# Four small reorderings in a routed MLP-and-adapter kernel: the first rows' turns, a split result sum, tail sums by matmul, two more unused products

## The reference

```
q, k, v = x@Wq, x@Wk, x@Wv ; attn = softmax(q k^T / 16) ; a = (attn v)@Wp + bp
cms     = gelu(a@cW1 + cb1)@cW2 + cb2 + one_hot(code)          # 256 -> 1024 -> 256
mod     = gelu([a, cms]@mW1 + mb1)@mW2 + mb2                    # 512 -> 1024 -> 256
x1      = clip(x + cms + mod, 0, 1)
for layer in 3 adapters:   # weights chosen by the batch's role, 3 roles
    u  = gelu(x@W_down[role] + b_down)@W_up[role] + b_up        # 256 -> 128 -> 256
    x  = layernorm(x + u) * gamma[role] + beta[role]
```

## Time and profile before

| | |
|---|---|
| timed runs | 366.13 us median (365.42 to 367.71) |
| profiled execution | 363.89 us, its span 362.1 us |
| TensorE matmul busy | 348.7 us, 96% of the span |
| TensorE weight load | 282.9 us, 78% |
| VectorE | 197.0 us, 54% |
| ScalarE | 166.4 us, 46% |
| GpSimd | 62.0 us, 17% |
| granted TensorE clock | 9 (full) in all 40 slices |
| busy tenths of TensorE, first and last slice | 7 and 4, 9 in nearly all between |

### The profile page before, as it was taken

One profiled execution on the slowest core, in us unless ns is written; L12 is line 12 of the kernel. 1 busy time (PEld: TensorE's weight loads), 2 busy tenths in 40 slices (PEclk: granted clock), 3 DMA queues, 4 the chain that ended last, 5 costly groups with the idle time before them and its releaser, 6 DMA issues.

```text
span 362.1 us, 6606 instructions
## 1 busy us (share of the span) xinstructions
PE 348.7 (96%) x2232; PEld 282.9 (78%) x2232; DVE 197.0 (54%) x477; ACT 166.4 (46%) x333; POOL 62.0 (17%) x94
## 2 busy tenths in 40 slices
PE   7889999999999999999999999999999999999994
PEld 6677688677876867888786777877899999989962
DVE  5057365420332746763535766554579777553584
ACT  3465685432652555452326454443455554533421
POOL 2700230000040101001311111003322025100231
PEclk9999999999999999999999999999999999999999
DMA  6663799175020223220076797602856543298001
GB/s 209 202 229 119 200 106 162 11 213 130 2 58 0 60 80 97 69 79 0 29 242 159 208 264 241 172 29 80 207 151 191 160 107 98 66 295 310 16 2 44
DMA packets 30646, 46.14 MB, mean 127 GB/s; under 512 B 4779, under 2 KB 15348, under 8 KB 30612
## 3 DMA queue, kind: packets, MB, share of 16 engines
q1 hardware_dynamic: 28852, 41.72, 42.6%
q0 software_dynamic: 1392, 3.80, 3.6%
q10 hardware_dynamic: 368, 0.20, 0.2%
HBM read 43.60 MB, written 4.48 MB: 133 GB/s over the span
## 4 chain that ended last, share of the span: by engine, by line
PE 85%; ACT 5%; DVE 4%; issue 3%; POOL 2%; DMA 1%; POOLq 0%; DVEq 0%; ACTq 0%
PE bank L312 11%; PE bank L314 10%; PE bank L313 10%; PE bank L1353 8%; PE bank L1358 8%; PE bank L1354 7%; PE bank L1277 4%; PE bank L1397 4%; PE bank L1376 3%; PE bank L1228 2%; PE bank L1267 2%; PE bank L1248 2%; ACT h_full L760 2%; PE bank L1428 2%; ACT h_hi L764 1%
## 5 line engine op out<-in xcount | busy, mean ns | idle before, releaser
L760 ACT ACTIVATE h_full<-bank,bias 128x512 f32<-128x512 f32 (+1 forms) x80 | 48.2, 602 | 114.4 <-PE bank L314 109.6
L985 DVE TENSOR_TENSOR h_lo<-h_full,h_hi 128x512 fp32r<-128x512 f32 (+1 forms) x80 | 46.7, 584 | 65.1 <-ACT h_hi L764 63.6
L683 POOL TENSOR_TENSOR rstd<-moments,minus_half 128x1 f32<-128x1 f32 x39 | 24.3, 624 | 174.2 <-DVE moments L1039 174.2
L764 ACT ACTIVATE h_hi<-h_full 128x512 fp32r<-128x512 f32 (+1 forms) x80 | 43.7, 546 | 2.6
L1031 DVE TENSOR_TENSOR window_y<-bank,window_x 128x256 f32<-128x256 f32 x39 | 16.5, 423 | 42.6 <-PE bank L1376 34.8
L1353 PE MATMUL bank<-h_hi,m_hi 128*128 128x512 f32 (+1 forms) x80 | 31.1, 397 | 0.4 <-ACT h_hi L764 0.3
L1353 PE MATMUL bank<-h_hi,c_hi 128*128 128x512 f32 (+1 forms) x80 | 30.8, 395 | 0.1
L312 PE MATMUL bank<-at_hi,m_hi 128*128 128x512 f32 (+1 forms) x80 | 29.5, 369 | 0.0
L312 PE MATMUL bank<-at_hi,c_hi 128*128 128x512 f32 (+1 forms) x80 | 29.4, 367 | 0.0
L314 PE MATMUL bank<-at_lo,c_hi 128*128 128x512 f32 (+1 forms) x80 | 27.8, 348 | 0.0
L314 PE MATMUL bank<-at_lo,m_hi 128*128 128x512 f32 (+1 forms) x80 | 27.8, 347 | 0.0
(11 more groups left out here) (216 smaller groups left out, 717.9 us busy)
## 6 DMA issues: line engine op xcount, KB each, us to landing
adapter_w<-packed_w SPq DMA_DIRECT2D x48, 256.5 KB, 3.5
adapter_rows<-packed_rows SPq DMA_DIRECT2D x36, 256.0 KB, 3.7
mixed_w<-packed_w SPq DMA_DIRECT2D x12, 256.5 KB, 4.6
stage<-in_L_cond_mW SPq DMA_DIRECT2D x6, 512.0 KB, 4.7
stage<-in_L_cond_cW SPq DMA_DIRECT2D x4, 512.0 KB, 6.5
last_w<-packed_w SPq DMA_DIRECT2D x2, 769.5 KB, 5.8
up_bias<-in_L_cond_b_up SPq DMA_DIRECT2D x12, 128.0 KB, 5.5
adapter_rows<-packed_rows SPq DMA_DIRECT2D x24, 64.0 KB, 3.2
```

The source lines that it names most:

```text
L683: pool.tensor_tensor(slot.rstd[:, :], slot.moments[:, 1:2], minus_half[:, :], ALU.pow)\
L760: act.activation(h_full[:, n % 2, rows], bank[n % 2][:, rows], ACT.Gelu, bias=bias[:, b:b + 1])\
L764: act.activation(h_hi[:, n % 2, rows], h_full[:, n % 2, rows], ACT.Copy).then_inc(h_hi_ready, 1)
L985: dve.tensor_tensor(h_lo[:, n % 2, rows], h_full[:, n % 2, rows], h_hi[:, n % 2, rows].bitcast(F32), ALU.subtract).then_inc(h_lo_ready, 1)
```

## The change

- In `core`, `D 7` comes right behind `D 6`; before, `Ha 8` stood between them. `C` is one place earlier for that.
- In the start, `half_part("X", 0)` comes ahead of `fold_weights(1)` and the bias turn, and `half_part("X", 1)` ahead of `half_part("Y", 0)`, on TensorE and ScalarE. `keep_busy(1)` is added ahead of the wait for `earlier_ready`, and the one of 64 columns becomes one of 128.
- Group 2's `F` and `E` run in two halves of 256 rows (F, E, F, E), so `x1_needed` of windows 8 and 9 asks for the first half only. Counts of `mod_summed` and `x1_ready` change to suit.
- Tails: `last_sum` on VectorE is gone. TensorE puts `up_bias` into the sum bank with an identity product (`last_bias`), `last_first_sum` is two plain products with the identity as the moving side that add to it, and layer 0's `last_residual` is gone. Tail one's `last_bias`, `last_first_sum` and `last_down` stand behind `Hb 9` of group 4, ahead of `D 8`; before, the latter two stood behind `D 8`.

```diff
-        core += [("D", HB - 2), ("Ha", HB), ("D", HB - 1), ("C", 0), ("Ha", HB + 1), ("Hb", HB), ("Hb", HB + 1)]
+        core += [("D", HB - 2), ("D", HB - 1), ("C", 0), ("Ha", HB), ("Ha", HB + 1), ("Hb", HB), ("Hb", HB + 1)]
...
+        def sum_parts(g):
+            return 2 if g + 1 in CARRIED and GROUPS[g][1] == GR else 1
+        def summed(g):
+            return VB * sum(sum_parts(n) for n in range(g))
...
+            n, (first, rows) = next((n, group) for n, group in enumerate(GROUPS) if (w + 1) * P <= sum(group))
+            part = ((w + 1) * P - first - 1) * sum_parts(n) // rows
+            return PRIMED + summed(n) + VB * (part + 1)
...
+                if step in ("F", "E"):
+                    share = size // sum_parts(g)
+                    for part_n in range(sum_parts(g)):
+                        rows = slice(part_n * share, (part_n + 1) * share)
...
-            def last_sum(tail):
-                dve.wait_ge(tail.loaded, 16 * tail.loads)
-                dve.wait_ge(tail.turned, 1)
...
-                dve.tensor_tensor(tail.x[:, :], tail.sum_bank[:, 0:V], tail.up_bias[:, :], ALU.add).then_inc(tail.x_ready, 1)
...
             keep_busy(2)
...
             pe.matmul(bank[4][0:B, 0:1], role_row[:, 1, :], ones[0:1, 0:1], start=True, stop=True).then_inc(roles_turned, 1)
+            keep_busy(1)
             pe.wait_ge(earlier_ready, 1)
...
-            keep_busy(1, P // 2)
+            keep_busy(1)
...
+            def last_bias(n):
+                tail = last[n]
+                pe.wait_ge(tail.loaded, 16 * tail.loads)
+                pe.matmul(tail.sum_bank[:, 0:V], ident[:, :], tail.up_bias[:, :], start=True, stop=False)
...
-                    ins = pe.transpose(tail.sum_bank[:, vb * P:(vb + 1) * P], xT[:, vb, columns(w)], ident[:, :])
-                ins.then_inc(tail.turned, 1)
+                    pe.matmul(tail.sum_bank[:, vb * P:(vb + 1) * P], xT[:, vb, columns(w)], ident[:, :],
+                              start=False, stop=False)
...
+            half_part("X", 0)
             pe.wait_ge(wT_copied, 3)
...
-            half_part("X", 0)
+            half_part("X", 1)
             half_part("Y", 0)
-            half_part("X", 1)
             half_part("Y", 1)
...
-                if g == NM - 1 and step == ("D", HB):
+                if g == NM - 1 and step == ("Hb", HB + 1):
                     pe.wait_ge(cms_copied, VB * NM)
-                    pe.wait_ge(last[0].loaded, 16 * last[0].loads)
+                    last_bias(0)
                     pe.wait_ge(x1_ready, x1_needed(LAST[0]))
+                    last_first_sum(0)
                     last_down(0, 0)
-                    last_first_sum(0)
                 if g == NM - 1 and step == ("D", HB + 2):
-                    last_residual(0, 0)
                     last_up(0, 0)
```

More of the change, by code:

```diff
@@ L467, in go @@
             def go():
-                engine.wait_ge(tail.x_ready, tail.base + LAYERS + 1)
+                engine.wait_ge(tail.x_ready, tail.base + LAYERS)
                 for q, place in zip(quarters, places):
@@ L806, in last_part @@
                 if stage_name == "turn":
-                    act.wait_ge(tail.turned, layer + 1)
+                    act.wait_ge(tail.turned, layer)
                     act.activation(tail.xT[:, :, :], two(tail.turn_bank[:, 0:V]), ACT.Copy).then_inc(tail.xT_ready, 1)
@@ L1007, in part @@
                     dve.wait_ge(base_ready, VB * (g + 1))
[L1008 to L1015, removed]
+                if step in ("F", "E"):
+                    share = size // sum_parts(g)
+                    for part_n in range(sum_parts(g)):
+                        rows = slice(part_n * share, (part_n + 1) * share)
+                        cols = slice(first + part_n * share, first + (part_n + 1) * share)
+                        if step == "F":
+                            for vb in range(VB):
+                                dve.scalar_tensor_tensor(cms[:, vb, rows], result_banks(g, HB)[vb][:, rows],
+                                                         bias[:, MB2 + vb:MB2 + vb + 1], xT[:, vb, cols], ALU.add, ALU.add)\
+                                    .then_inc(mod_summed, 1)
+                        if step == "E" or sum_parts(g) > 1:
+                            for vb in range(VB):
+                                dve.wait_ge(mod_summed, summed(g) + VB * part_n + vb + 1)
+                                dve.tensor_scalar(xT[:, vb, cols], cms[:, vb, rows], 0.0, 1.0, ALU.max, ALU.min)\
+                                    .then_inc(x1_ready, 1)
             def before(wave, spot):
@@ L1078, in last_norm @@
                 dve.wait_ge(tail.rstd_ready, tail.base + layer + 1)
+                if layer == 0 and tail.left:
+                    dve.wait_ge(*tail.left)
                 dve.scalar_tensor_tensor(tail.x[:, :], tail.y[:, :], tail.rstd[:, :], tail.rows[layer][:, 1, :],
@@ L1099, in _ @@
                     part("E", 0, g - 1)
-                if g + 1 in CARRIED and step == ("F", 0):
+                if g + 1 in CARRIED and step == ("F", 0) and sum_parts(g) == 1:
                     part("E", 0, g)
@@ L1173, in _, with keep_busy @@
             pe.wait_ge(ident_ready, 1)
-            def keep_busy(n, columns=P):
+            def keep_busy(n):
                 for _ in range(n):
-                    pe.matmul(bank[6][:, 0:columns], ident[:, :], ident[:, 0:columns], start=True, stop=True)
+                    pe.matmul(bank[6][:, 0:P], ident[:, :], ident[:, :], start=True, stop=True)
             keep_busy(2)
@@ L1446, in last_residual @@
                 tail = last[n]
-                pe.wait_ge(tail.x_ready, tail.base + layer + 1)
+                pe.wait_ge(tail.x_ready, tail.base + layer)
                 pe.matmul(tail.sum_bank[:, 0:V], ident[:, :], tail.x[:, :], start=True, stop=False)
@@ L1517, in _ @@
             last_down(one, 1)
+            pe.wait_ge(gelu_done, PRIMED + 2 * HB * NM)
+            last_bias(two_)
             last_up(one, 1)
-            pe.wait_ge(x1_ready, PRIMED + VB * NM)
-            pe.wait_ge(gelu_done, PRIMED + 2 * HB * NM)
+            last_bias(three)
+            pe.wait_ge(x1_ready, PRIMED + summed(NM))
             pe.wait_ge(emptied[6], used[6])
@@ L1523, in _ @@
             for n in (two_, three):
-                pe.wait_ge(last[n].loaded, 16 * last[n].loads)
                 last_down(n, 0)
                 last_first_sum(n)
-            for n in (two_, three):
-                last_residual(n, 0)
-                last_up(n, 0)
+            last_up(two_, 0)
+            last_up(three, 0)
             last_turn(one, 2)
```

23 lines of the change are left out of this document (8 added, 15 removed).

## The result

The change made the kernel slower: 369.45 us median (368.74 to 369.86, four executions) against 365.77 us (365.00 to 367.71) of the kernel before on the same chip, a ratio of 1.0113 with an interval of 1.0071 to 1.0155 (the medians alone give 1.010). Forecast was 367.6, in a range to 369.8. The profiled execution took 369.24 us, span 367.4, where that of before took 363.89 and 362.1: +5.3 us between the two profiles. The mean granted clock of TensorE is 0.982 to 0.987 in all four executions; in the profile of before it was 1.00.

What follows compares the result with a forecast made beforehand. TensorE's work plus its gaps was taken as the bound (85% of the last chain). Terms +0.8 + 0.3 - 0.5 - 0.2 + 1.4 - 0.4 + 0.1 gave +1.5 us on the median 366.13: 367.6 us, range 365.1 to 369.8.

Steps and rivals of the forecast that it cites:

- start, order: First turn to first scores: the second fold no longer hides behind the gather, +0.8 us, bounds 0 and +2.1.
- tail one's entry: Group 4: the bias product ahead of `D 8` waits for the last of tail one's loads, +1.4 us.
- start: order and unused products: Start up to the first scores: new order +0.8 us and added unused products +0.3 us.
- `D 7` ahead of `Ha 8`: Group 0: `cms` leaves its banks earlier, so TensorE's wait at `Hb 8` shrinks, -0.5 us; nothing in other groups.
- `F` and `E` in halves: End of group 2: window 8's down product no longer waits, but a wait returns later, -0.2 us.
- residual gone: Group 4: the residual product that goes from `D 10` gives -0.4 us.
- tails: Tails: two bias products come in and VectorE's three sums go, +0.1 us, bounds -0.3 and +0.4.
- +0.3 for the added products: Start: widened and new unused products delay the work ahead of the gather, +0.3 us, bounds 0 and 0.6.
- rival 4: Start, 11.9 to 15.2 us: the clock falls in the new gap, middle 370.4 us, chance 0.14.
- Rival 3: Start: added products make the clock rise sooner and more surely, up to 2.2 us off, 365.4 us, chance 0.14.
- the wait of group 2 returns inside `D 1`: Group 2: the low part comes later, so `D 1`'s last two products wait, about 0.5 us.
- Theory F: Follow-up theory: TensorE's clock falls to 1.2 GHz behind idle stretches over 2 us, ahead of first turn and tail one's bias product.

Runs made afterwards that it cites:

- the order put back: The changed kernel with both folds ahead of the first turn again, as before the change; ratio to the kernel before 1.0024 (0.9989 to 1.0060).
- the stretch filled: The changed kernel with nine more unused products of 128 columns ahead of the first turn; ratio to the kernel before 1.0031 (1.0001 to 1.0060).
- the order alone: The kernel before with only the first turn moved ahead of the second fold; ratio to the kernel before 1.0056 (1.0010 to 1.0101).
- both put back: The changed kernel with the start's old order and tail one's products behind `D 8` again; ratio to the kernel before 1.0029 (0.9996 to 1.0062).

## Why the prediction was wrong

Its sum was for one clock, and the change moves the clock: the terms "start, order" and "tail one's entry" failed. Step by step, by how much later the same product starts in the profile after:

| step | forecast | profile |
|---|---|---|
| start: order and unused products | +1.1 | +2.37 |
| `D 7` ahead of `Ha 8` | -0.5 | -0.61 |
| late low part in group 2 | none | +0.90 |
| `F` and `E` in halves | -0.2 | -0.27 |
| group 3, cause not traced | none | -0.28 |
| tail one's entry | +1.4 | +3.46 |
| residual gone | -0.4 | -0.42 |
| tails | +0.1 | +0.13 |
| sum | +1.5 | +5.3 |

- **"Start, order"** failed: "What TensorE does in place of the fold, from 11.9 to 14.5, is nothing" was costed at nothing, but the clock fell in that stretch. It cost the fold 1.63 us (3.62 less 1.99) and, from start to start, 2.6 us in all from the first turn to the first scores. The order itself cost 0.1 us and not 0.8: the sum added the lengths of rows (0.66, 1.99, 3.98), which overlap; the distances between starts are 0.49, 1.82 and 3.46. And the gather landed 0.35 us earlier in this execution. 2.6 + 0.1 - 0.35 is the +2.37: the overpriced order and the early gather hid part of what the clock cost. The +0.3 for the added products can't be told from the gather's spread (where the first turn waits for it, it starts between 13.2 and 14.9 us over the profiles).
- It was rival 4, "the clock falls in the new gap", given 0.14 at 370.4; the kernel came out at 369.45. That nearness is partly luck: the rival counted a fall in the start alone, which explains 1.27 us beyond the forecast; 2.06 more come from tail one's entry. Its price of one fold, +1.4, was low as well, since the first fold of before ran at both levels (records of 379 to 793 ns). Against it I had put that small products shorten the gap. The added products did the opposite: the first fold ended sooner in this execution (10.86, not 11.3), which made the gap longer.
- **"Tail one's entry"** had the mechanism right, a wait on the last of seven loads that no engine releases. Forecast for it were 1.6 us; it was 2.18, as the load took 6.0 us to land. What failed is the sum behind it, "bias product 0.45, first sum 0.45, down 0.45", at full speed: I weighed the rule of the Trainium skill for the start alone and not for the second idle stretch that the change makes. 1.5 of the 3.46 us are clock. In two profiles without a fall there (the order put back, the stretch filled) the same step costs 1.6 us, close to the +1.4.
- **The base.** I took the profile's 1.00 as the kernel's clock. Over 110 executions it is 0.995, a loss of nearly 2 us. Rival 3 had seen the 2.24 us between profile and median and read them as something that the change could win. The change went the other way, to 0.987.
- At a constant clock the forecast was, if anything, too high: the rests of the two runs of the change (with its own and with the old unused products) are +0.7 and -0.1 us against +1.5, and without the 0.7 us too much for the order it would have been +0.8.
- `D 7`, the halves, the residual and the tails came within 0.11 us. That the wait of group 2 returns inside `D 1` was right, at 0.28 us and not 0.5. The late load of group 2 varies by execution: the same step is between -0.1 us (the order alone) and +1.1 us (both put back) in other profiles. The -0.28 us of group 3 are in every profile of a changed kernel and in none of the variants of the kernel before.

## What to carry to other kernels

An edit that lets TensorE stand idle can cost twice: the wait, and then the work behind it at the lower clock level (here a fold of 3.62 us and not 1.99). So price the clock's fall at every place where a change makes a new idle stretch, and read the mean clock of many executions, not of one profile. If the stretch is surely idle, unused products in it can pay (0.7% here); if a load makes it, issue that load first in its queue and give it a semaphore of its own. A product moved ahead of others must not take a wait for all of a group's loads along with it. And add up distances between starts, not lengths of rows that overlap.

## What the runs showed of the hardware that was not expected

- The clock fell in, or up to 0.9 us behind, idle stretches of 1.35 to 3.52 us (2.67 and 2.18 in the profile after, 1.63 in the order alone), and did not at others of 1.80, 1.85, 2.62 and 3.02 us: the same place falls in one execution and not in the next, and the length alone doesn't tell, so the "over 2 us" of Theory F isn't borne out. In the profile after, a fall cost the work behind it 2.6 us in the start and 1.5 us at tail one.
- It also fell with TensorE busy in every window, near 60 us, behind 24 one-column products in a row (2.73 us), in six of thirteen profiles, and in none of the three in which they stood in two halves.
- Two more unused products ahead of the first fold went with a clock that rose sooner: the fold took 1.99 or 2.00 us in seven of eleven profiles with them and never under 2.52 in five without. The time gained nothing, as the gather behind it landed no sooner.
- One load of one size (`up_bias`, 128 KB) landed in 3.2 us when it was issued first and in 5.5 and 6.0 us as the last of seven.
